# First attention of a four-layer Flamingo stack: the keys of a pair's first context are made at steps 4 to 6 of the pair ahead instead of steps 8 to 10

## The reference

```python
Qp = query @ Wq + bq                     # query: layer-normed x
K = _l2norm(key @ Wk + bk)               # key = value = ctx_768, 1500 rows of 96 per batch
V = value @ Wv + bv
Q = _l2norm(Qp)                          # both split into 16 heads of 8
scores = jnp.einsum('bhqd,bhkd->bhqk', Q, K) * SCALE
attn = jax.nn.softmax(scores, axis=-1)
out = jnp.einsum('bhqk,bhkd->bhqd', attn, V)
out = out.transpose(0, 2, 1, 3).reshape(B, Nq, EMBED_DIM) @ Wo + bo
```

## Time and profile before

| | |
|---|---|
| median of 3 runs | 5338.53 us |
| the profiled execution | 5341.67 us, of which the span of the core is 5340.1 us |
| first attention, first to last exponential | 297 us to 1043 us of the span |
| busy share of the span | PE 75%, DVE 49%, ACT 41%, POOL 22% |
| mean granted TensorE clock of the profiled run | 0.85 |

### The profile page before, as it was taken

The page is one execution under the profiler, slowest core; times in us unless marked ns, Lnnn a source line. Parts: engine busy times, 40 slices in busy tenths (PEclk is TensorE's granted clock), DMA queues, the critical chain, the costliest instruction groups (busy, mean ns, idle before and its releaser), DMA issues. The chain is left out here.

```text
span 5340.1 us, 86460 instructions
## 1 busy us (share of the span) xinstructions
PE 3979.1 (75%) x32916; PEld 2573.6 (48%) x32916; DVE 2617.3 (49%) x2823; ACT 2165.2 (41%) x2795; POOL 1190.4 (22%) x1506
## 2 busy tenths in 40 slices
PE   6388888826369999989999642218859688888885
PEld 6256666513136666546666310017623255555553
DVE  6522222242234444144442257664443698888983
ACT  5256666501013332313333125864421365555552
POOL 0111111120312232133222000001100655444520
PEclk8689999968669999979999765559979799899997
DMA  4155555315322222022221023000000555555530
GB/s 123 52 121 117 129 112 125 83 58 182 94 62 57 63 68 64 20 72 69 67 64 46 11 60 86 0 0 1 2 14 0 121 126 130 123 134 117 132 93 12
DMA packets 142965, 401.94 MB, mean 75 GB/s; under 512 B 31977, under 2 KB 45211, under 8 KB 142614
## 3 DMA queue, kind: packets, MB, share of 16 engines
q1 hardware_dynamic: 111518, 352.58, 26.1%
q0 software_dynamic: 26624, 44.18, 3.7%
q10 hardware_dynamic: 4608, 2.10, 0.1%
HBM read 238.40 MB, written 8.09 MB: 46 GB/s over the span
## 5 line engine op out<-in xcount | busy, mean ns | idle before, releaser
L1816 DVE TENSOR_REDUCE L_mp<-ps 112x2 f32<-112x1000 f32 x384 | 458.3, 1199 | 699.0 <-PE ps L1700 699.0
L1801 ACT ACTIVATE L_p<-ps 125x896 f32<-125x896 f32 x384 | 352.2, 917 | 872.8 <-PE ps L1725 801.0
L1737 PE MATMUL ps<-L_p,L_cn 125*97 125x448 f32 x1536 | 639.2, 538 | 0.0
L2452 DVE TENSOR_REDUCE L_mp<-ps 112x2 f32<-112x1000 f32 x384 | 456.9, 1194 | 126.9 <-PE ps L2253 114.2
L2417 ACT ACTIVATE L_p<-L_p 125x896 f32<-125x896 f32 x384 | 364.6, 950 | 261.9 <-DVE L_p L2469 261.8
L2469 DVE SCALAR_TENSOR_TENSOR L_p<-ps,L_lb 125x896 f32<-125x896 f32 x384 | 415.0, 1081 | 19.5 <-DMA L_lb<-L_low 10.0
L879 ACT ACTIVATE L_p<-ps,rk 125x896 f32<-125x896 f32 x384 | 385.0, 1008 | 79.8 <-PE ps L761 77.4
L1723 PE MATMUL ps<-L_qh,L_ch 97*125 97x448 f32 x768 | 401.1, 522 | 13.4 <-DMA L_qh<-L_mc 13.4
L1737 PEld LDWEIGHTS ps<-L_p,L_cn 125*97 125x97 f32 x1536 | 250.4, 163 | 205.7 <-issue 165.9
L2285 PE MATMUL ps<-L_p,L_vs 125*32 125x112 f32 x6144 | 241.1, 277 | 109.6 <-ACT L_p L2417 94.5
L2253 PE MATMUL ps<-L_ks,L_qs 96*128 96x500 bf16 x768 | 250.6, 413 | 73.7 <-DMA L_ks<-L_k_part 45.1
(11 more groups left out here) (489 smaller groups left out, 7103.0 us busy)
## 6 DMA issues: line engine op xcount, KB each, us to landing
L_ks<-L_k_part SPq DMA_DIRECT2D x288, 375.0 KB, 7.7
L_ks<-L_k_first SPq DMA_DIRECT2D x96, 375.0 KB, 5.8
moe_w<-in_L_w SPq DMA_DIRECT2D x64, 512.0 KB
L_cn<-in_ctxN SPq DMA_DIRECT2D x32, 568.4 KB
cs_ct<-in_ctxT SPq DMA_DIRECT2D x32, 562.5 KB, 4.3
L_ct<-in_ctxT SPq DMA_DIRECT2D x32, 562.5 KB, 4.6
L_raw<-in_ctxT SPq DMA_DIRECT2D x32, 562.5 KB
L_cr<-in_ctxT POOLq DMA_DIRECT2D x32, 562.5 KB, 4.7
```

The costliest lines, as they stand in the source:

```text
L1737: mm = nc.tensor.matmul(U[:, a, :], CN[s][:, j, :], P[:, n % 2, a * HALF:(a + 1) * HALF], start=(j == 0), stop=(j == KT - 1))
L1801: nc.scalar.activation(two(P[:, n % 2, :]), SB[n % 2], ACT.Exp).then_inc(S["exped"].sem, 1)
L1816: nc.vector.tensor_reduce(mp[:, 2 * k:2 * k + 2], ps[0:TT, bank:bank + 2, 0:500], AX.X, ALU.max).then_inc(S["chunk_maxed"].sem, 1)
L2452: nc.vector.tensor_reduce(mp[:, 2 * c:2 * c + 2], ps[0:TT, CB[pair], 0:500], AX.X, ALU.max).then_inc(S["chunk_maxed"], 1)
```

## The change

The three chunks of keys of the pair ahead's first context are issued at PE's steps 4, 5 and 6 of the pair instead of 8, 9 and 10. As all engines take their order from `key_steps`, ACT's `first` goes from steps 10, 11, 12 to 6, 7, 8 and its `second` from 11, 12, 13 to 7, 8, 9; DVE's `rest_of_keys` goes ahead of the copies of the values of steps 7 to 10, with which it alternated. SP's and POOL's programs are not changed. No instruction and no byte is added or taken away.

```diff
@@ -581,7 +581,7 @@
     S = {n: core.sig(f"{L}_{n}").sem for n in NAMES}
-    KEYS0, KEYS1 = (8, 9, 10), (18, 19, 20)
+    KEYS0, KEYS1 = (4, 5, 6), (18, 19, 20)
     VALUES1, VALUES0 = (7, 8, 9, 10), (16, 18, 20, 22)
```

## The result

The changed kernel takes 5430.86 us (median of 4 runs, 5424.99 to 5438.47) against 5339.66 us: 1.0172 times as long, 95% interval 1.0154 to 1.0190. That is +91 us; 5421 us had been forecast, in a range of 5372 to 5450.

The account below looks back on a forecast made before the run. The first attention was taken as bound by the loop over one set of key part buffers. Its four terms, 14.5 + 13.95 + 14.5 + 10.6 = 53.55 us a pair against 47.73, gave +83 us: 5421 us, range 5372 to 5450.

Parts of the forecast that it names:

- The loop: First attention: one set of kparts closes a loop of making and placing keys, four terms without slack, 47.8 us a pair.
- P1: Placing of context 1's keys to the next `first`: stays 14.5 us, so step 6 waits for it.
- K0: `first` of context 0 to its placing: from 9.5 to 13.95 us, bounds 11.9 and 15.3.
- P0: Placing of context 0's keys to the `first` of context 1: from 12.8 to 14.5 us, load directly ahead.
- The gain: At step 20: the wait for the placing shrinks by 0.7 us and stays at about 5.
- K1: `first` of context 1 to its placing: keeps its steps, 10.6 us taken, bounds 8.3 and 11.8.
- rival B: The clock stays up after one or both waits: 5392 us, or 5361 with both; 9%.
- The sum: All four terms of the loop: 53.55 us a pair against 47.73, +5.8 us, 14 times.
- the first pair: Start of the stage, before the 14 counted periods: its `first` of 335.38 comes at 336.5 to 338.5, +2 us.
- A: Rival: a placing lands before ACT asks for it, so no wait; faster, to 5250 us; 3%.
- C: Rival: the third part, not step 10, starts context 0's placing; no change, 5331 us; 5%.

Follow-up runs that it names:

- two_sets: Changed kernel with a second set of three part buffers, for context 1: 5233.03 us, ratio 0.9802 to the kernel before; repeated, 5236.85 us, 0.9822.
- two_sets_before: Kernel before (keys at steps 8 to 10) with the second set of part buffers: 5239.51 us, ratio 0.9829; repeated, 5239.91 us, 0.9824.
- place_first: Changed kernel with SP placing context 0's keys before it waits for step 10's values and loads context 1: 5406.03 us, ratio 1.0130 to the kernel before.
- warm: Changed kernel with one key product computed five more times where PE stands at step 6, pairs 1 to 14: 5402.81 us, ratio 1.0124 to the kernel before.
- load_late: Kernel before with context 1's load delayed until the third parts are there, directly ahead of context 0's placing: 5376.58 us, ratio 1.0081.
- before: The kernel before the change, keys at steps 8 to 10 with one set of part buffers: 5339.66 us.
- keys_10: Kernel before with the keys of context 0 at steps 10 to 12: 5378.39 us, ratio 1.0084.

## Why the prediction was right

- **The loop, and what was hidden.** P1 can't start earlier and isn't covered by six steps: `first` at step 6 costs ACT 8.18 us of idle time and PE 5.33 (4.9 forecast). Right, and `two_sets` with `two_sets_before` shows it as the cause: without the waits for the placing the same change of steps costs nothing.
- **K0 +4.4 us.** 14.1 in the mean after, 13.95 forecast; `place_first` shows that step 10's values end it (10.35 without them), `warm` that the clock is 1.7 us of it (2.1 counted).
- **P0 +1.7 us.** 14.6 in the mean after, 14.5 forecast; `load_late` shows the load as the cause, with 1.9 in the mean.
- **The gain.** From weighing 11 to the `first` of step 20 it is 556.02 - 540.70 = 15.3 us (15.45 forecast, 16.1 before). So this stretch of the loop shrank as said, but the wait in it did not, although I had forecast that too (ACT 5.66 against 5.73 us, PE 3.75 against 3.82): PE's steps in between took 557.55 - 3.75 - 540.70 = 13.1 us instead of 13.86. Of these 0.76 us some 0.58 are the wait for the copy of sums ahead of weighing 12, which is gone with keys at steps 4 to 6. In the loop that is worth nothing, since the landing ends this stretch.
- **K1.** The one term that was mis-sized by its reason: 10.6 us taken, 10.88 in the mean, the same as before. I had PE stand 3.1 us at step 20 and a shorter slow stretch behind it. PE stood 3.75 us in the row shown, and 3.8 us in the mean of the stage, as before; and the granted clock was down behind it (0.50 from 557 to 562 us), as before. The lower bound of K1 was also a slip: 10.96 less 2.5 is 8.5, not 8.3. With it the farther price of rival B is 5363 us instead of 5361.
- **The sum.** 54.15 - 47.73 = 6.4 us a pair instead of 5.8. Of the 0.6 us K1 has 0.28, K0 0.16, P0 0.11 and P1 0.05, 8 us over the 14 pairs; and the first pair is at +4.4 instead of +2, since its first placing landed 0.7 us later than counted (310.8) and its P0 was 15.3. The stage is then 94 us longer, up to the `first` of 1097.88 against 1003.53. The profiled execution, 5424.99 us, is only 83 us over that of before; the rest, some 11 us, comes back behind that row, in stages that the change doesn't touch, and the medians (+91) don't have it. The two traces show where: 10 of the 11 us lie in the last attention, whose exponentials (L2417) run from 4229.2 to 5224.7 us before and from 4322.7 to 5308.0 after. The same code took from 980.4 to 995.5 us in the twelve traces of this study, and the kernel before has the longest. Two runs of one kernel differ as well, 992.6 and 984.2 us in `two_sets` and its repetition. So it is the spread of one stage from execution to execution; what makes it was not tested. That 5425 was forecast for the profiled execution and 5424.99 measured is therefore luck: two errors of 11 us met.
- **Rivals.** A (the placing lands in time) is out: P1 was 14.6 us. B (the clock stays up) did not come by itself, but `warm` made it come at step 6. Its price was 29 us, measured 26. C (the third part starts the placing) is out, and `place_first`, which lets SP place before the load, shows that its 5331 us was too low twice: it forgot the load, which then comes behind and is late, and its K0 of 9.1 us forgot the wait for the scores of step 9. The third parts were there 9.0 us after the `first` (531.44 - 522.45), as counted, but the scores only at 532.68, and K0 was 10.35.

## What to carry to other kernels

Where a buffer has one copy, add up the terms of the loop that it closes (fill, transfer, fill, transfer) and set them against the period: if they agree (47.8 and 47.73 us here), the loop sets the pace, and making something earlier only moves a wait for the buffer's last reader earlier, to where less work covers it. Ask first which work covers a transfer, and then what stands ahead of the next transfer in its queue. The way out is a second copy of the buffer, as far as possible in memory that is idle in that stage: 9 KB a partition, of which 6 KB were such memory, brought 1.8 to 2.0%, while no place of the steps with one set came under the kernel before.

## What was not expected of the hardware

A load of 562 KB queued behind six transfers of 375 KB landed 9.1 us after its issue (538.85 to 547.92, `place_first`) instead of the 4.5 us of the kernel before (the median of its loads from 345 to 1000 us), and the same load less than 1 us ahead of them delayed their landing by 1.9 us in the mean (`load_late`). With the load 3.1 us ahead (`before`) or 7.4 us ahead (`keys_10`) the placing took 12.8 us. So in this kernel the order of a queue and the distance in it both count, and the question is which of the two transfers is waited for first. And PE did more work in less time: 5 products more in each pair, 26 us less in all.
